# The ternary feed-forward stage of an eight-layer kernel: the batch loop written out, both middle layers with output tiles innermost, each batch's last layer issued between the next batch's first tiles

## The chip, the cores and the metric

One core of one Trainium2 chip runs the whole program once. The metric is the device time of that one launch in microseconds (us); lower is better. The data type of every matmul in the stage at hand is fp32.

## What is computed

The program is a sequence of eight layers with a residual and a layernorm behind each: four attention-like layers and four feed-forward layers, on x of 4 batches of 512 positions with 128 channels. The stage that the diff touches is the second of the eight, the first feed-forward (its weights are -1, 0 or 1 times a factor, but are used here as plain fp32):

```python
def _tlin(x, w, s):
    return jnp.einsum('bsi,oi->bso', x, w) * s
h = jax.nn.silu(_tlin(x, w1_w, w1_s)) * _tlin(x, w2_w, w2_s)     # 128 -> 512
h = jax.nn.gelu(_tlin(h, h1_w, h1_s), approximate=False)         # 512 -> 512
h = jax.nn.gelu(_tlin(h, h2_w, h2_s), approximate=False)         # 512 -> 512
return _tlin(h, w3_w, w3_s)                                      # 512 -> 128
...
x = _layernorm(x + _L0_ffn_ref(x, ...), axis=-1)
```

## The kernel before

`build` (at the end of the file) runs the stages one behind another; each stage is a block of its own in which every engine has one instruction stream, and a block ends when all its engines are done. Between two stages stands `layernorm`, a block too, in which SyncE also loads the next stage's weights. So the ternary stage begins when the layernorm before it has written X, and the next layernorm begins when the ternary stage has written the last batch of R.

Channels lie on the 128 partitions and the 512 positions of a batch along the free dimension. X is the stage's input and also the residual, R its output. The 512 hidden channels are four tiles of 128 (`HT` is 4), counted by m for an output tile and by k for an input tile. PSUM is `c.ps`, eight banks of 128x512 fp32; every matmul fills one bank with 128x512.

For each batch b, in a `Fori` loop on each of three engines (L182, L206, L221):

- First layers (L187, L188): for m = 0 to 3 one matmul with w1 into bank 2m and one with w2 into bank 2m+1. ScalarE takes the silu of bank 2m into G (L209), and VectorE multiplies bank 2m+1 by its scale and by G into H1 (L225).
- First middle layer (L195, `layer` 0): TensorE waits for all four H1 tiles, and then makes output tile m by four matmuls over k in a row, into bank m. ScalarE takes the gelu of each output tile into H2 (L214).
- Second middle layer (L195 again, `layer` 1): TensorE waits for all four H2 tiles; output tile m goes to bank 4+m, its gelu to H3 (L214).
- Last layer (L200): TensorE waits for all four H3 tiles; four matmuls over k into bank 0. VectorE scales this and adds X into R (L228). The next batch's first matmul writes bank 0, and so TensorE waits for L228 (the wait at the top of its loop, which for batch 0 is satisfied by the `sem_inc` at L219).

That makes 8 + 16 + 16 + 4 = 44 matmuls a batch and 176 in the stage. The order of each engine is the order of the program text; nothing is planned or reordered. Semaphore `tiles` counts finished output tiles of TensorE, `act_done` ScalarE's activations, `dve_done` VectorE's products; in the loops their target values are computed from the loop's register b. SyncE's part in the stage is four DMAs that write blanks into `da_bands` (L176) for the stage that follows.

The relative attention (its first block entry below is L1700) and the other attention stages don't share code with this one. `hashed_ffn`, `lowrank_ffn` and others are written without `Fori`; `rwkv_attention` has one.

Of the kernel before, what the change touches and what calls it, by code (L numbers as in the profile page):

```python
# [15 lines left out]
ALU = mybir.AluOpType  # L16
# [3 lines left out]
P = 128  # L20
B, T = 4, 512
N = B * T
PAD = 3
# [119 lines left out]
def ternary_ffn(c):  # L143

    d = c.dram
    H = 512
    HT = H // P
    loaded, tiles = c.sem("tf_loaded"), c.sem("tf_tiles")
    act_done, dve_done = c.sem("tf_act_done"), c.sem("tf_dve_done")
    TILES, ACTS, DVES = 2 * HT + 2 * HT + 1, 3 * HT, HT + 1  # L150
    SPAN, ROW = 64, 256
    c.bands = [[c.nc.dram_tensor(f"da_bands{i}{j}", (UNITS * P * ROW,), F32, kind="Internal").ap() for j in range(2)] for i in range(2)]
    with ExitStack() as ctx:
        w1 = c.sb("tf_w1", [P, H], ctx)
        w2 = c.sb("tf_w2", [P, H], ctx)
        h1 = c.sb("tf_h1", [P, HT, H], ctx)
        h2 = c.sb("tf_h2", [P, HT, H], ctx)
        w3 = c.sb("tf_w3", [P, HT, P], ctx)
        s = c.sb("tf_s", [P, 4 * HT + 1], ctx)
        G = c.sb("tf_G", [P, HT, T], ctx)  # L160
        H1 = c.sb("tf_H1", [P, HT, T], ctx)
        H2 = c.sb("tf_H2", [P, HT, T], ctx)
        H3 = c.sb("tf_H3", [P, HT, T], ctx)
        pairs = [(w1[:, :], d["tf_w1"]), (w2[:, :], d["tf_w2"]), (s[:, :], d["tf_s"]), (h1[:, :, :], d["tf_h1"]),
                 (h2[:, :, :], d["tf_h2"]), (w3[:, :, :], d["tf_w3"])]
        yield [(loaded, pairs)]
        block = c.block(ctx)

        @block.sync
        def _(eng):  # L170
            eng.wait_ge(loaded, 16 * len(pairs))
            blank = c.X[:, 0, PAD + T:PAD + T + SPAN].unsqueeze(1).to_broadcast([P, UNITS, SPAN])
            for pair in c.bands:
                for side, buf in enumerate(pair):
                    dst = bass.AP(buf.tensor, buf.offset + (ROW - SPAN) * side, [[ROW, P], [P * ROW, UNITS], [1, SPAN]])
                    eng.dma_start(dst, blank).then_inc(loaded, 16)  # L176
            eng.wait_ge(loaded, 16 * (len(pairs) + 4))

        @block.tensor
        def _(eng):  # L180
            eng.wait_ge(loaded, 16 * len(pairs))
            with eng.Fori(0, B) as b:  # L182
                x = c.X[:, b, PAD:PAD + T]
                eng.wait_ge(dve_done, b * DVES + 1)
                for m in range(HT):
                    cols = slice(m * P, (m + 1) * P)
                    eng.matmul(c.ps[:, 2 * m, :], w1[:, cols], x, start=True, stop=True).then_inc(tiles, 1)  # L187
                    eng.matmul(c.ps[:, 2 * m + 1, :], w2[:, cols], x, start=True, stop=True).then_inc(tiles, 1)  # L188
                eng.wait_ge(dve_done, b * DVES + HT + 1)
                for layer, (w, hid) in enumerate(((h1, H1), (h2, H2))):  # L190
                    if layer:
                        eng.wait_ge(act_done, b * ACTS + 2 * HT)
                    for m in range(HT):
                        for k in range(HT):
                            mm = eng.matmul(c.ps[:, 4 * layer + m, :], w[:, k, m * P:(m + 1) * P], hid[:, k, :],  # L195
                                            start=k == 0, stop=k == HT - 1)
                        mm.then_inc(tiles, 1)
                eng.wait_ge(act_done, b * ACTS + 3 * HT)
                for k in range(HT):
                    mm = eng.matmul(c.ps[:, 0, :], w3[:, k, :], H3[:, k, :], start=k == 0, stop=k == HT - 1)  # L200
                mm.then_inc(tiles, 1)

        @block.scalar
        def _(eng):
            eng.wait_ge(loaded, 16 * len(pairs))
            with eng.Fori(0, B) as b:  # L206
                for m in range(HT):
                    eng.wait_ge(tiles, b * TILES + 2 * m + 1)
                    eng.activation(G[:, m, :], c.ps[:, 2 * m, :], ACT.Silu, scale=s[:, m:m + 1]).then_inc(act_done, 1)  # L209
                for layer, out in enumerate((H2, H3)):  # L210
                    for m in range(HT):
                        eng.wait_ge(tiles, b * TILES + 2 * HT + layer * HT + m + 1)
                        k = (2 + layer) * HT + m
                        eng.activation(out[:, m, :], c.ps[:, 4 * layer + m, :], ACT.Gelu, scale=s[:, k:k + 1])\  # L214
                           .then_inc(act_done, 1)

        @block.vector
        def _(eng):
            eng.sem_inc(dve_done, 1)  # L219
            eng.wait_ge(loaded, 16 * len(pairs))  # L220
            with eng.Fori(0, B) as b:  # L221
                for m in range(HT):
                    eng.wait_ge(tiles, b * TILES + 2 * m + 2)
                    eng.wait_ge(act_done, b * ACTS + m + 1)
                    eng.scalar_tensor_tensor(H1[:, m, :], c.ps[:, 2 * m + 1, :], s[:, HT + m:HT + m + 1], G[:, m, :],  # L225
                                             ALU.mult, ALU.mult).then_inc(dve_done, 1)
                eng.wait_ge(tiles, b * TILES + TILES)
                eng.scalar_tensor_tensor(c.R[:, b, :], c.ps[:, 0, :], s[:, 4 * HT:4 * HT + 1], c.X[:, b, PAD:PAD + T],  # L228
                                         ALU.mult, ALU.add).then_inc(dve_done, 1)


def hashed_ffn(c):
# [2438 lines left out]


LAYERS = [delta_attention, ternary_ffn, relative_attention, hashed_ffn, rwkv_attention, lowrank_ffn, rotary_attention, routed_ffn]


# [155 lines left out]
```

## Time and profile before

| what | value |
|---|---|
| median of 3 runs | 3025.05 us (3017.87 to 3030.14) |
| the profiled execution's own time | 3023.27 us |
| its span | 3021.3 us |
| mean granted TensorE clock over the span | 0.867 |
| TensorE busy over the whole span | 2375.7 us, 79% |
| VectorE, ScalarE busy | 2157.8 us, 1549.6 us |
| the ternary stage, first matmul to last residual | 1343.7 to 1516.5 us |

The span is the time between the first and the last instruction that the profile shows; the execution's own time is 2.0 us above it. All positions below are in us from the span's start. "PE" is TensorE's matmul, "PEld" its weight load, "DVE" VectorE, "ACT" ScalarE, and PEq or DVEq the instruction queue of an engine, where register and semaphore instructions are seen. One fp32 matmul of the source appears as two MATMUL instructions (two passes), each with its weight load, so the 44 matmuls of a batch are 88 passes.

### The profile page before, as it was taken

To read this page: it belongs to the slowest core of one execution; us is meant where nothing else is said; L and a number is where in the kernel's file an instruction comes from. 1 tells how busy PE (TensorE), PEld (TensorE's weight loads), DVE (VectorE), ACT (ScalarE), POOL (GpSimd) and SP (SyncE) were. 2 spreads that over 40 slices of the span, in tenths; PEclk is the share of its full clock that TensorE was granted. 3 is DMA by queue.
4 is the path that set the end of the run, shared out by engine and by line. 5 is a ranking of instruction groups with operands and counts; after the bars stand their busy time and mean duration, and the time that the engine had idled before them with its cause. 6 is when DMAs were issued, how large, how long until landed. Compare 5 with 4: busy or idle time off the path is not lost. (4 is left out here: it accounts for less than half of the span.)

```text
span 3021.3 us, 63536 instructions
## 1 busy us (share of the span) xinstructions
PE 2375.7 (79%) x25313; PEld 1626.9 (54%) x25365; DVE 2157.8 (71%) x3992; ACT 1549.6 (51%) x3982; POOL 270.2 (9%) x280
## 2 busy tenths in 40 slices
PE   6778877787777877769938999998867766778677
PEld 5667777676676766743315666665322221222366
DVE  6999999999999999940035777787256656665465
ACT  3555555566556656652235777776311132556434
POOL 0000000000000000000031010100022311110242
PEclk9887788888887878889968999999988887999888
DMA  5111110111111111020039999994100001110421
GB/s 174 30 30 30 30 30 23 24 30 30 30 30 30 30 30 30 16 67 0 0 89 232 246 231 239 238 236 119 35 0 0 0 23 57 40 40 26 156 70 63
DMA packets 200035, 214.28 MB, mean 71 GB/s; under 512 B 32150, under 2 KB 185766, under 8 KB 194310
## 3 DMA queue, kind: packets, MB, share of 16 engines
q1 hardware_dynamic: 197353, 205.39, 25.9%
q0 software_dynamic: 2400, 4.95, 0.5%
q8 instruction: 199, 3.26, 0.5%
q14 instruction: 83, 0.68, 0.1%
HBM read 138.16 MB, written 74.74 MB: 70 GB/s over the span
## 5 line engine op out<-in xcount | busy, mean ns | idle before, releaser
L1274 DVE TENSOR_REDUCE ra_top<-ps 128x1 f32<-128x512 f32 x256 | 161.1, 683 | 97.7 <-PE ps L1078 91.3
L2594 DVE TENSOR_REDUCE dl_ZO<-dl_XP 128x64 f32<-128x128 f32 (+6 forms) x448 | 219.7, 490 | 15.4
L2590 DVE TENSOR_TENSOR dl_XP<-dl_ZO,dl_G 128x64 f32<-128x64 f32 (+6 forms) x448 | 194.6, 434 | 15.4
L1772 ACT ACTIVATE da_AB<-ps 128x384 f32<-128x384 f32 x256 | 124.5, 490 | 147.0 <-PE ps L1634 143.4
L1195 ACT ACTIVATE ra_PT<-ps 128x512 f32<-128x512 f32 x256 | 136.6, 598 | 117.3 <-PE ps L1097 116.6
L1928 DVE TENSOR_TENSOR ps<-ps,da_window 128x192 f32<-128x192 f32 (+1 forms) x256 | 101.2, 395 | 122.3 <-PE ps L1657 118.0
L1782 ACT ACTIVATE da_E<-ps,da_top 128x512 f32<-128x512 f32 x256 | 176.1, 688 | 17.4 <-DVE da_top L1931 16.9
L1931 DVE TENSOR_REDUCE da_top<-ps 128x1 f32<-128x512 f32 x256 | 177.0, 691 | 8.8
L1664 PE MATMUL ps<-ident,da_E 128*128 128x128 f32 x1024 | 169.1, 288 | 1.3 <-ACT da_E L1782 1.2
L2165 PE MATMUL ps<-X,dl_taps_q 128*128 128x128 f32 x1088 | 148.9, 304 | 2.2 <-DVE dl_taps_q L2655 2.2
L2165 PEld LDWEIGHTS ps<-X,dl_taps_q 128*128 128x128 f32 x1088 | 145.7, 220 | 4.2 <-DVE dl_taps_q L2655 2.4
L2223 PE MATMUL ps<-dl_kqN,dl_ST 64*64 64x32 f32 x4096 | 114.6, 282 | 40.4 <-DVE dl_ST L2614 36.6
L1473 POOL MEMSET da_K<- 32x4096 f32 x2 | 7.1, 3573 | 1528.9 <-POOLq L82 1528.9
L2165 PE MATMUL ps<-X,dl_taps_k 128*128 128x128 f32 x1088 | 143.1, 297 | 0.0
L2165 PEld LDWEIGHTS ps<-X,dl_taps_k 128*128 128x128 f32 x1088 | 140.0, 213 | 1.0
L1664 PEld LDWEIGHTS ps<-ident,da_E 128*128 128x128 f32 x1024 | 108.4, 141 | 50.4 <-issue 39.9
L2223 PEld LDWEIGHTS ps<-dl_kqN,dl_ST 64*64 64x64 f32 x4096 | 109.9, 210 | 46.0 <-issue 45.6
L2165 PEld LDWEIGHTS ps<-X,dl_taps_v 128*128 128x128 f32 x1088 | 126.1, 193 | 13.1 <-issue 9.5
L2431 ACT ACTIVATE dl_FB<-dl_F,dl_beta_now 128x32 f32<-128x32 f32 x512 | 126.7, 351 | 9.8 <-DVE dl_F L2499 9.8
L2165 PE MATMUL ps<-X,dl_taps_v 128*128 128x128 f32 x1088 | 126.0, 275 | 3.3 <-DVE dl_taps_v L2655 2.3
L2581 DVE TENSOR_TENSOR dl_ZO<-dl_ZO,dl_aT 128x32 f32<-128x32 f32 (+6 forms) x448 | 128.0, 286 | 0.0
L1078 PE MATMUL ps<-ra_KS,ra_QS 128*128 128x512 bf16 x246 | 103.3, 424 | 23.3 <-DMA ra_QS<-ra_zero 22.7
(403 smaller groups left out, 5766.6 us busy)
## 6 DMA issues: line engine op xcount, KB each, us to landing
da_bands<-da_AB SPq DMA_DIRECT2D x128, 384.0 KB, 3.8
dl_Abc<-dl_ends SPq DMA_DIRECT2D x64, 512.0 KB, 6.3
da_window<-da_bands SPq DMA_DIRECT2D x128, 192.0 KB, 4.4
da_across<-da_bands SPq DMA_DIRECT2D x128, 192.0 KB, 4.5
da_parts<-da_split SPq DMA_DIRECT2D x64, 96.0 KB, 3.3
rf_We<-in_rf_We SPq DMA_DIRECT2D x1, 4608.0 KB, 23.0
da_K<-da_parts SPq DMA_DIRECT2D x16, 256.0 KB
da_Q<-da_parts SPq DMA_DIRECT2D x16, 256.0 KB
```

Of the source, the lines that this page charges most:

```text
L1195: eng.activation(PT[:, k % 2, h, :], ps[:, tscore_bank(UNITS * m + v), :], ACT.Exp).then_inc(s["exps"], 1)
L1274: eng.tensor_reduce(top[:, m % 2, u:u + 1], ps[:, score_bank(UNITS * m + u), :], AXX, ALU.max, negate=True).then_inc(s["maxima"], 1)
L1664: mm = eng.transpose(ps[:, 2 + U % 2, k * P:(k + 1) * P], E[:, U % 2, k * P:(k + 1) * P], c.ident[:, :])
L1772: eng.activation(AB[:, j % STAGES, h, :, :], ps[:, band_bank(v), 0:2 * BAND].rearrange("p (k x) -> p k x", k=2), ACT.Copy)\
L1782: eng.activation(E[:, U % 2, :], ps[:, score_bank(U), :], ACT.Exp, bias=top[:, u:u + 1], accum_out=total[:, m % 2, u:u + 1]).then_inc(s["e ...
L1931: eng.tensor_reduce(top[:, u:u + 1], bank, AXX, ALU.max, negate=True).then_inc(s["maxima"], 1)
L2165: mm = eng.matmul(out, taps[w][:, tap, cols], columns_of(c.X, m, tap), start=tap == 0, stop=tap == TAPS - 1)
L2223: mm = eng.matmul(starts_ps[e][DK * (h ^ w):DK * (h ^ w) + DK, w, pair // 2, :], ST[rows, pair, :], kqN[rows, pair, e * CH:(e + 1) * CH, : ...
L2431: ins = eng.activation(FB[:, e, :, t // SB, t % SB], F[:, e, :, t // SB, t % SB], ACT.Copy, scale=beta_now[:, 1, t:t + 1])
L2581: link(eng.tensor_tensor(mine[:, :, 0:t], mine[:, :, 0:t], aT[:, e, :, u, t + 1].unsqueeze(2).to_broadcast([P, I, t]), ALU.mult))
L2590: link(eng.tensor_tensor(XP[:, :, :, SB - t:], seen.unsqueeze(1).to_broadcast([P, 2, I, t + 1]), G[:, x:x + 2, keys][:, ::-1, :].unsqueeze ...
L2594: link(eng.tensor_reduce(ZO[:, to:to + 1 + (2 * I - 1) * CH:CH].rearrange("p (k i) -> p k i", k=2), XP[:, :, :, SB - 1 - t:], AXX, ALU.add))
```

## The change

The batch loop of all three engines is a Python loop now, so it is written out four times, and every wait has a constant, looked up in the tables `tile`, `acts` and `dves` that are filled in the order in which the engines issue. In the two middle layers the loop over k is the outer one and the loop over the output tiles m the inner one: all four banks of a layer are open at once, each gets its matmul of k = 0, then each that of k = 1, and so on, and the wait stands ahead of each k. The first layers' tiles are taken in the order 0, 1, 3, 2. The last layer of batch b-1 is issued behind the first layers' tiles 0 and 1 of batch b, into bank 4 instead of bank 0, and its residual likewise on VectorE; tile 2 of the first layers, whose banks are 4 and 5, stands behind a wait for that residual.

```diff
--- before.py
+++ after.py
@@ -147,7 +147,22 @@
     HT = H // P
     loaded, tiles = c.sem("tf_loaded"), c.sem("tf_tiles")
     act_done, dve_done = c.sem("tf_act_done"), c.sem("tf_dve_done")
-    TILES, ACTS, DVES = 2 * HT + 2 * HT + 1, 3 * HT, HT + 1
+    ORDER = (0, 1, 3, 2)
+    tile, acts, dves = {}, {}, {}
+    for b in range(B):
+        for m in ORDER:
+            if m == 3 and b:
+                tile["out", b - 1] = len(tile) + 1
+                dves["out", b - 1] = len(dves) + 1
+            for side in range(2):
+                tile["first", b, m, side] = len(tile) + 1
+            acts["silu", b, m] = len(acts) + 1
+            dves["gated", b, m] = len(dves) + 1
+        for layer in range(2):
+            for m in range(HT):
+                tile["hidden", b, layer, m] = len(tile) + 1
+                acts["gelu", b, layer, m] = len(acts) + 1
+    tile["out", B - 1] = len(tile) + 1
     SPAN, ROW = 64, 256
     c.bands = [[c.nc.dram_tensor(f"da_bands{i}{j}", (UNITS * P * ROW,), F32, kind="Internal").ap() for j in range(2)] for i in range(2)]
     with ExitStack() as ctx:
@@ -178,55 +193,71 @@
 
         @block.tensor
         def _(eng):
+            def first(b, m):
+                cols = slice(m * P, (m + 1) * P)
+                for side, w in enumerate((w1, w2)):
+                    eng.matmul(c.ps[:, 2 * m + side, :], w[:, cols], c.X[:, b, PAD:PAD + T], start=True, stop=True).then_inc(tiles, 1)
+
+            def hidden(b, layer, w, hid, ks):
+                for i, k in enumerate(ks):
+                    if layer == 0:
+                        eng.wait_ge(dve_done, dves["gated", b, ks[max(i, 1)]])
+                    else:
+                        eng.wait_ge(act_done, acts["gelu", b, 0, k])
+                    for m in range(HT):
+                        mm = eng.matmul(c.ps[:, 4 * layer + m, :], w[:, k, m * P:(m + 1) * P], hid[:, k, :], start=i == 0, stop=i == HT - 1)
+                        if i == HT - 1:
+                            mm.then_inc(tiles, 1)
+
+            def last(b):
+                eng.wait_ge(act_done, acts["gelu", b, 1, HT - 1])
+                for k in range(HT):
+                    mm = eng.matmul(c.ps[:, 4, :], w3[:, k, :], H3[:, k, :], start=k == 0, stop=k == HT - 1)
+                mm.then_inc(tiles, 1)
+
             eng.wait_ge(loaded, 16 * len(pairs))
-            with eng.Fori(0, B) as b:
-                x = c.X[:, b, PAD:PAD + T]
-                eng.wait_ge(dve_done, b * DVES + 1)
-                for m in range(HT):
-                    cols = slice(m * P, (m + 1) * P)
-                    eng.matmul(c.ps[:, 2 * m, :], w1[:, cols], x, start=True, stop=True).then_inc(tiles, 1)
-                    eng.matmul(c.ps[:, 2 * m + 1, :], w2[:, cols], x, start=True, stop=True).then_inc(tiles, 1)
-                eng.wait_ge(dve_done, b * DVES + HT + 1)
-                for layer, (w, hid) in enumerate(((h1, H1), (h2, H2))):
-                    if layer:
-                        eng.wait_ge(act_done, b * ACTS + 2 * HT)
-                    for m in range(HT):
-                        for k in range(HT):
-                            mm = eng.matmul(c.ps[:, 4 * layer + m, :], w[:, k, m * P:(m + 1) * P], hid[:, k, :],
-                                            start=k == 0, stop=k == HT - 1)
-                        mm.then_inc(tiles, 1)
-                eng.wait_ge(act_done, b * ACTS + 3 * HT)
-                for k in range(HT):
-                    mm = eng.matmul(c.ps[:, 0, :], w3[:, k, :], H3[:, k, :], start=k == 0, stop=k == HT - 1)
-                mm.then_inc(tiles, 1)
+            for b in range(B):
+                for m in ORDER:
+                    if m == 3 and b:
+                        last(b - 1)
+                    if m == 2 and b:
+                        eng.wait_ge(dve_done, dves["out", b - 1])
+                    first(b, m)
+                hidden(b, 0, h1, H1, ORDER)
+                hidden(b, 1, h2, H2, range(HT))
+            last(B - 1)
 
         @block.scalar
         def _(eng):
             eng.wait_ge(loaded, 16 * len(pairs))
-            with eng.Fori(0, B) as b:
-                for m in range(HT):
-                    eng.wait_ge(tiles, b * TILES + 2 * m + 1)
+            for b in range(B):
+                for m in ORDER:
+                    eng.wait_ge(tiles, tile["first", b, m, 0])
                     eng.activation(G[:, m, :], c.ps[:, 2 * m, :], ACT.Silu, scale=s[:, m:m + 1]).then_inc(act_done, 1)
                 for layer, out in enumerate((H2, H3)):
                     for m in range(HT):
-                        eng.wait_ge(tiles, b * TILES + 2 * HT + layer * HT + m + 1)
+                        eng.wait_ge(tiles, tile["hidden", b, layer, m])
                         k = (2 + layer) * HT + m
                         eng.activation(out[:, m, :], c.ps[:, 4 * layer + m, :], ACT.Gelu, scale=s[:, k:k + 1])\
                            .then_inc(act_done, 1)
 
         @block.vector
         def _(eng):
-            eng.sem_inc(dve_done, 1)
+            def residual(b):
+                eng.wait_ge(tiles, tile["out", b])
+                eng.scalar_tensor_tensor(c.R[:, b, :], c.ps[:, 4, :], s[:, 4 * HT:4 * HT + 1], c.X[:, b, PAD:PAD + T],
+                                         ALU.mult, ALU.add).then_inc(dve_done, 1)
+
             eng.wait_ge(loaded, 16 * len(pairs))
-            with eng.Fori(0, B) as b:
-                for m in range(HT):
-                    eng.wait_ge(tiles, b * TILES + 2 * m + 2)
-                    eng.wait_ge(act_done, b * ACTS + m + 1)
+            for b in range(B):
+                for m in ORDER:
+                    if m == 3 and b:
+                        residual(b - 1)
+                    eng.wait_ge(tiles, tile["first", b, m, 1])
+                    eng.wait_ge(act_done, acts["silu", b, m])
                     eng.scalar_tensor_tensor(H1[:, m, :], c.ps[:, 2 * m + 1, :], s[:, HT + m:HT + m + 1], G[:, m, :],
                                              ALU.mult, ALU.mult).then_inc(dve_done, 1)
-                eng.wait_ge(tiles, b * TILES + TILES)
-                eng.scalar_tensor_tensor(c.R[:, b, :], c.ps[:, 0, :], s[:, 4 * HT:4 * HT + 1], c.X[:, b, PAD:PAD + T],
-                                         ALU.mult, ALU.add).then_inc(dve_done, 1)
+            residual(B - 1)
 
 
 def hashed_ffn(c):
```

## Rows read from the trace of the kernel before

**Rows 1.** Page of the profile: span, TensorE over the span.
```profile
span 3021.3 us, 63536 instructions
PE 2375.7 (79%) x25313; PEld 1626.9 (54%) x25365; DVE 2157.8 (71%) x3992; ACT 1549.6 (51%) x3982; POOL 270.2 (9%) x280
```
**Rows 2.** Busy time by window: window, length, then busy us and (instructions); PEclk granted clock.
```profile
1343.70:1349.80 6.10, 6.08 (x8) 2.51 (x9) 0.75 (x1) 2.30 (x3) 0.00 (x0) 0.51 0.86 193
1474.10:1516.70 42.60, 38.83 (x88) 16.39 (x88) 3.75 (x5) 9.53 (x13) 0.00 (x0) 1.00 0.00 0
```
**Rows 3.** Waits, 1330 to 1530: who waited for whom, total us, times, longest.
```profile
DVE R L228 <- PE ps L200: 134.3, 4, 33.6
ACT tf_H L214 <- PE ps L195: 95.1, 32, 3.8
PE ps L187 <- DVEq L219: 5.9, 1, 5.9
PE ps L1700 <- PEq L82: 5.5, 1, 5.5
```
**Rows 4.** Timeline, all engines, batch 0 to batch 1: start, length, instruction, idle before.
```profile
1343.72 2.07 PE L187 MATMUL ps<-X,tf_w 128*128 x2 [5.86 <-DVEq L219]
...
1352.80 1.02 PE L188 MATMUL ps<-X,tf_w 128*128 x2
...
1354.75 14.00 PE L195 MATMUL ps<-tf_H,tf_h 128*128 128x512 f32 x32 [0.93 <-DVE tf_H L225]
...
1383.57 0.69 ACT L214 ACTIVATE tf_H<-ps,tf_s 128x512 f32<-128x512 f32 x1 [2.75 <-PE ps L195]
1384.27 1.28 ACT L209 ACT_TABLE_LOAD   x1
1384.31 3.70 PE L200 MATMUL ps<-tf_H,tf_w 128*128 128x512 f32 x8 [0.78 <-ACT tf_H L214]
1388.28 0.75 DVE L228 SCALAR_TENSOR_TENSOR R<-ps,tf_s,X 128x512 f32 x1 [33.59 <-PE ps L200]
1389.19 1.12 PE L187 MATMUL ps<-X,tf_w 128*128 x2 [1.18 <-DVE R L228]
```
**Rows 5.** Timeline, TensorE, end of batch 2, batch 3 and the exit.
```profile
1469.29 3.70 PE L200 MATMUL ps<-tf_H,tf_w 128*128 128x512 f32 x8 [0.78 <-ACT tf_H L214]
1474.14 1.12 PE L187 MATMUL ps<-X,tf_w 128*128 x2 [1.16 <-DVE R L228]
1475.10 1.02 PE L188 MATMUL ps<-X,tf_w 128*128 x2
...
1480.25 1.02 PE L188 MATMUL ps<-X,tf_w 128*128 x2
1482.20 14.00 PE L195 MATMUL ps<-tf_H,tf_h 128*128 128x512 f32 x32 [0.93 <-DVE tf_H L225]
1496.98 14.00 PE L195 MATMUL ps<-tf_H,tf_h 128*128 128x512 f32 x32 [0.78 <-ACT tf_H L214]
1511.76 3.70 PE L200 MATMUL ps<-tf_H,tf_w 128*128 128x512 f32 x8 [0.78 <-ACT tf_H L214]
1515.71 0.75 DVE L228 SCALAR_TENSOR_TENSOR R<-ps,tf_s,X 128x512 f32 x1 [33.57 <-PE ps L200]
```
**Rows 6.** Timeline, TensorE, recurrent stage: spread (L826) and gather (L830) matmuls in turn.
```profile
2290.35 1.02 PE L830 MATMUL ps<-rw_rS,rw_gather 128*128 128x512 f32 x2
2291.20 1.02 PE L826 MATMUL ps<-rw_rkv,rw_spread 128*128 128x512 f32 x2
2292.06 1.02 PE L830 MATMUL ps<-rw_rS,rw_gather 128*128 128x512 f32 x2
```
**Rows 7.** Busy time by window, in three stages that are written out.
```profile
500.00:520.00 20.00, 15.69 (x419) 14.89 (x422) 18.78 (x38) 7.70 (x29) 0.00 (x0) 0.84 0.01 2
2114.70:2118.00 3.30, 3.25 (x4) 1.50 (x5) 0.00 (x0) 1.12 (x1) 0.00 (x0) 0.54 0.00 0
2463.00:2466.00 3.00, 3.00 (x5) 1.01 (x3) 1.47 (x2) 0.00 (x0) 0.00 (x0) 0.52 0.00 0
```

## What the change does to the time, predicted before it was run

> **What bounds the kernel now.** I read the page first: TensorE is busy 79% of the span [rows 1], but that is a mean over eight stages, so it says nothing of this one. The windows over the stage come next: a batch takes some 42.5 us and TensorE is busy for 38.83 of them, VectorE for 3.75 and ScalarE for 9.5 to 10.8 [rows 2] (batches 1 and 2 have the same numbers as batch 3). TensorE is the engine that sets the end, and the other two have room for a delay of many microseconds. The waits name large sums, 134.3 us of VectorE and 95.1 us of ScalarE [rows 3]; these are idle times of engines that don't bound, and they cost nothing. What costs is the short list of waits in which TensorE stands, and the timeline shows where: four times a batch, always where one layer needs the last tile of the layer before.
>
> **The unit.** In a run of first-layer passes 12 passes go from 1475.10 to 1480.25 [rows 5], 0.429 us each. The stage's 88 passes a batch are 37.75 us of the 42.5; the rest, 4.7 us, is stall. I measure every stall as start of a phase to start of the next, less the phase's passes at 0.429, so that the slightly longer first pass behind a stall is counted with it.
>
> **What goes away, stall by stall.**
> 1. First layers to first middle layer. Batch 3: 1474.14 to 1482.20 is 8.06, less 16 passes (6.86) is 1.20 [rows 5]. In batch 0 the last pair starts at 1352.80, its slot ends at 1353.66, and the next phase starts at 1354.75: 1.09 [rows 4]. Four of them: 1.09 + 3 x 1.20 = 4.69. Afterwards this layer begins with k = 0, whose product comes two tiles earlier, and needs the last-made tile (k = 2) only after 24 passes or 10.3 us.
> 2. First to second middle layer: 1482.20 to 1496.98 is 14.78, less 32 passes (13.73) is 1.05 [rows 5]. Four: 4.20. With m innermost the output tiles are finished in the last four matmuls, 0.86 apart. ScalarE's gelu takes 0.69 [rows 4], so it keeps up; tile 0's gelu ends some 1.7 us before the last tile is done (3 x 0.86 earlier, plus 0.2 and 0.69), and the next layer starts without a pause. The gelu of tile 3 is needed 12 matmuls (10.3 us) later.
> 3. Second middle layer to last layer: again 14.78, 1.05 [rows 5]. Three of the four go, as the last layer of batch b-1 stands behind four matmuls (3.43 us) of batch b; that of batch 3 has no next batch and stays.
> 4. Last layer to the next batch. From 1384.31 to 1389.19 is 4.88, less 8 passes (3.43) is 1.45 [rows 4]; from 1469.29 to 1474.14 it is 1.42 [rows 5]. With 1.43 between them for the middle one, three make 4.30. This is the wait for the residual L228, which reads bank 0.
>
> Sum 4.69 + 4.20 + 3.15 + 4.30 = 16.3 us. The other way round: from 1353.66 there remain 336 passes, 144.1 us, plus one stall of 1.05; from the start of the last phase to the end of the residual it is 1511.76 to 1516.46, 4.70 [rows 5]. The residual would end at 1353.66 + 144.1 - 3.43 + 1.05 + 4.70 = 1500.1 instead of 1516.5, which is 16.4. I take 16.4.
>
> **Two small terms.** TensorE's idle time at the entry of the stage is 5.86 us, released by the queue of VectorE (the `sem_inc`), and 5.5 at the relative attention, a block without a loop [rows 3]; the layernorm before both is the same code. Without loop and `sem_inc` the entry should be 0.36 shorter. Its bounds are 0 and 0.36 and I take 0.36, since the row is the same code but for the loop. The residual starts 0.25 behind the end of the last pass (1511.76 + 3.70 to 1515.71) [rows 5], with register operations of the loop in between; I count 0.1 for these, between 0 and 0.25.
>
> **What is added, and what hides it.**
> - The residual of batch b-1 is now waited for ahead of tile 2. It ends 4.72 us after its last layer starts (1384.31 to 1389.03) [rows 4]; on TensorE the last layer (8 passes) and tile 3 (4 passes) take 12 x 0.429 = 5.15 us. That leaves 0.43 us, just one pass, by which a weight load runs ahead. So it is late by 0 to 0.1 us, three times: 0 to 0.3, and I take 0. Behind the waiting instruction stand only the batch's own tile 2 and its first middle layer.
> - ScalarE switches its table between gelu and silu, 1.28 us [rows 4]. The first silu of batch b can come no earlier than gelu, table and silu behind the second middle layer: about 0.2 + 0.69 + 1.28 + 0.69 = 2.9 us. Its product is needed at 10.3 us behind that point, so this is hidden; without cover it would cost its 1.28 once a batch.
> - The last layer waits for the gelu of tile 3, done about 1 us behind the second middle layer and needed 3.43 us behind it: 2.4 us of room.
> - Nothing is added in passes, weight loads or bytes. SyncE's four DMAs are untouched.
> - The written-out stream is longer. A written-out stage gives TensorE 419 matmuls in 20 us [rows 7], over 20 a microsecond, where this one needs 2.3. Its bounds are 0 and, as the loop's step back ends in a first matmul only 0.15 us behind the residual (1389.04 to 1389.19) [rows 4], a gain or loss of that size at each of three seams, 0.45 us. I take 0, as the denser stream is the nearer row.
> - Four open accumulation groups instead of one. The recurrent stage changes bank with each matmul while the gather in bank 2 (L830, `start=k == 0`) is still open: 2290.35, 2291.20, 2292.06, that is 0.86 for two passes, the same as within one bank [rows 6]. So 0, and no gain is possible either, as the passes are back to back already. The row has one open group and not four, which leaves rival C.
> - The clock at the entry. TensorE had been idle for 5.86 us and runs at 0.51 of full speed, the 1.2 GHz level, until about 1349.8, 6.1 us [rows 2]. Behind the same layernorm the hashed stage has 0.54 for only 3.3 us, and the low-rank stage is at 0.52 over 3 us after earlier slow ones [rows 7]. When it rises after the change can't be told from these rows; the stretch could be 3 us shorter, which gives 1.5 us back, or as much longer. I take 0.
>
> **A page that speaks against it.** The timeline shows gaps of 0.78 to 1.2 us in this stage and a granted clock of 1.00 for all of batch 3 [rows 2, 5]. The Trainium skill (TensorE: Matmul & The Clock Gate, section Loop structure matters more than you think) holds that the loop over k for one output tile should be the inner one so that TensorE stays warm, with the waits of the bad order being for DMAs of 8 us. The trace does not bear it out for this stage: there is no DMA in the loops, and the nest before kept its clock through all these gaps. What it would do here is rival E.
>
> **Sum.** 16.4 + 0.4 + 0.1 = 16.9 us off 3023.3, the profiled execution's own time (span 3021.3, [rows 1], and 2.0 around it): 3006.4. That execution was 1.8 below the median of the runs, so against the median 3025.05 the forecast is 3008.2, or -0.56%. All of it should reach the end: the next layernorm can't start before the last residual, and no transfer of the next stage is awaited there.
>
> **Rivals.**
> - A. Half of the stalls come back elsewhere: the residual wait is late and each last layer still stalls, so that stalls 3 and 4 (7.45 us) stay. For it: only 0.43 us of room. Against: the residual's own duration is fixed. 3008.2 + 7.5 = 3015.7.
> - B. The stage gives all of it, but the stages behind it give some back: they start 17 us earlier, with other clock and DMA phases. For it: runs of the very same program lie 12.3 us apart; against it: nothing in those stages refers to a fixed time. About half the spread, 6 to 10 us: 3014 to 3018.
> - C. Slower: with four groups open and the bank changing at each matmul, the weight load is no longer hidden behind the pass before. Its place is the 256 passes of the middle layers. A weight load takes 16.39 / 88 = 0.19 us [rows 2], so the price is 256 x 0.19 = 48.6 us, 3008.2 + 48.6 = 3057. It decides from 16.9 / 256 = 0.066 us a pass. For it: no row has four open groups. Against it: the alternating passes of [rows 6].
> - D. The change doesn't do what it says at the seam of the middle layers: the stall only moves, because the gelu of tile 0 is not done when the second middle layer starts. The room is 1.7 us, against it; for it speaks only that the gelus now come in a burst. Then 1.05 us stays four times: 3012.4.
> - E. TensorE falls to its 1.2 GHz level in the middle layers. A pass costs 0.429 more, 256 of them 110 us: 3118, and 39 such passes take the gain away. Against it: 1.00 granted in spite of larger gaps [rows 2]. The rule of the Trainium skill told above would make the time this.
>
> **Numbers.** Forecast 78%, A 6%, B 9%, C 2%, D 4%, E 1%. What a measurement can tell from no change is 0.5%, 15.1 us, so the line lies at 3009.9, only 1.7 us above the forecast, and three runs of the kernel before spread over 12.3 us. With some 5 us of scatter in the difference the forecast comes out below the line in 64% of its cases, 0.50; A, B and D give another 0.05. Faster 0.55. Slower 0.04: C and E, and 0.01 for a drift in the stages behind beyond B. Same 0.41. The range takes 5 to 6 us of scatter and the clock's 1.5 on the low side, and A, B and D on the high side: 3000 to 3019.
>
> **What would show it.** In the trace of the changed kernel: the middle layers' passes in one unbroken run of 0.429 each, also across the seam of the two; TensorE's idle time between 1354 and the last layer of batch 3 near 0, with one gap of 0.78 left in front of that last layer; entry idle 5.5; about 42.5 - 4.7 = 37.8 us a batch at a clock of 1.00; first matmul to last residual about 156.2 us instead of 172.7. The argument is wrong if passes in the middle layers take more than 0.43, if the clock falls below 1.00 inside the stage, or if a gap remains ahead of tile 2. It is right in the stage and wrong in the sum if the stage takes 156 us and the span is still above 3012.

## The result and the profile after

The changed kernel took 3004.43 us (median of six runs, 2997.9 to 3005.43), the kernel before 3025.66 us (3017.87 to 3032.14, also six): a ratio of 0.9926 with a 95% interval of 0.9908 to 0.9945, or 17 to 28 us less. The forecast was 3008.2 in a range of 3000 to 3019. The profiled execution has a span of 3003.6 us, 17.7 below the one before. Of all executions in this text one stands apart, an execution of e9 that took 5431 us; no trace of it exists, and the ratios leave it out.

The windows over the stage in the changed kernel (window, length, busy us of PE, PEld, DVE, ACT and POOL, granted clock, DMA share, GB/s) answer to [rows 2]. From the second window on TensorE is busy all the time, but for 1.9 us of the last one, where 38.83 of 42.6 us was the rule before. The granted clock is 0.50 at the entry and 1.00 from the first middle layer on:

```profile
1342.50:1346.00 3.50, 3.44 (x4) 1.50 (x5) 0.00 (x0) 1.30 (x2) 0.00 (x0) 0.50 0.66 148
1346.00:1349.80 3.80, 3.80 (x10) 1.77 (x9) 1.50 (x2) 2.04 (x3) 0.00 (x0) 0.96 0.88 199
1385.00:1426.80 41.80, 41.80 (x98) 18.43 (x98) 5.16 (x7) 11.96 (x16) 0.00 (x0) 1.00 0.00 0
1426.80:1464.60 37.80, 37.80 (x89) 16.72 (x88) 3.66 (x5) 10.74 (x15) 0.00 (x0) 1.00 0.00 0
1464.60:1498.00 33.40, 31.51 (x74) 13.56 (x73) 1.50 (x2) 7.03 (x11) 0.00 (x0) 1.00 0.00 0
```

The timeline of TensorE shows the two middle layers as one run of 64 passes, with no idle time behind it in three of four batches. From the start of such a run to the start of the next one on it takes 27.46 us (1351.36 to 1378.82), 0.429 a pass; the 27.63 of the line hold the last pass to its end. One gap is left, of 0.78 us, ahead of the last layer of batch 3; compare [rows 4, 5], where such a line stands at each change of layer. (The times are start and length; L199 is the first layers, L208 the middle ones, L215 the last.)

```profile
1342.56 8.96 PE L199 MATMUL ps<-X,tf_w 128*128 128x512 f32 x16 [5.50 <-PEq L82]
1351.36 27.63 PE L208 MATMUL ps<-tf_H,tf_h 128*128 128x512 f32 x64
1378.82 3.60 PE L199 MATMUL ps<-X,tf_w 128*128 128x512 f32 x8
1382.26 3.60 PE L215 MATMUL ps<-tf_H,tf_w 128*128 128x512 f32 x8
1385.69 3.60 PE L199 MATMUL ps<-X,tf_w 128*128 128x512 f32 x8
1389.12 27.63 PE L208 MATMUL ps<-tf_H,tf_h 128*128 128x512 f32 x64
...
1464.66 27.63 PE L208 MATMUL ps<-tf_H,tf_h 128*128 128x512 f32 x64
1493.06 3.70 PE L215 MATMUL ps<-tf_H,tf_w 128*128 128x512 f32 x8 [0.78 <-ACT tf_H L241]
1497.87 3.67 PE L95 MATMUL ps<-R,ones_mean 128*128 128x512 f32 x8 [1.11 <-PEq L168]
```

The same boundary on ScalarE and VectorE (L241 gelu, L236 silu, L258 product, L248 residual) shows what now runs while TensorE works. The gelus follow one another 0.86 us apart, the table switch comes while TensorE is in tiles 0 and 1, and the residual ends at 1386.64, before TensorE needs it for tile 2, four passes behind 1385.69, at 1387.41:

```profile
1378.16 0.69 ACT L241 ACTIVATE tf_H<-ps,tf_s 128x512 f32<-128x512 f32 x1 [0.17 <-PE ps L208]
1379.02 0.69 ACT L241 ACTIVATE tf_H<-ps,tf_s 128x512 f32<-128x512 f32 x1 [0.17 <-PE ps L208]
1379.73 1.28 ACT L236 ACT_TABLE_LOAD   x1
1381.02 1.26 ACT L236 ACTIVATE tf_G<-ps,tf_s 128x512 f32<-128x512 f32 x2
1385.89 0.75 DVE L248 SCALAR_TENSOR_TENSOR R<-ps,tf_s,X 128x512 f32<-128x512 f32 x1 [2.67 <-PE ps L215]
```

The waits over the same stretch (who waited for whom, total us, times, longest) answer to [rows 3]. VectorE's and ScalarE's large sums are still there, one of them under a new name (93.1 us for the silu), and cost as little as before:

```profile
DVE tf_H L258 <- ACT tf_G L236: 93.1, 4, 29.5
ACT tf_H L241 <- PE ps L208: 86.1, 32, 10.5
PE ps L199 <- PEq L82: 5.5, 1, 5.5
PE ps L215 <- ACT tf_H L241: 0.8, 1, 0.8
```

Cut at the first matmul of each layernorm (L95), the two profiled executions fall into nine parts (us):

| part | before | after |
|---|---|---|
| up to the first layernorm | 1330.76 | 1329.95 |
| **ternary stage with the layernorm ahead of it** | **186.02** | **167.92** |
| relative attention | 585.37 | 585.16 |
| hashed feed-forward | 67.88 | 69.75 |
| recurrent stage | 273.09 | 273.10 |
| low-rank stage | 24.46 | 24.78 |
| rotary attention | 348.23 | 344.85 |
| routed stage | 188.38 | 190.90 |
| last layernorm and store | 17.11 | 17.19 |

The ternary segment lost 18.1 us. The others moved by up to 3.4 us either way; in sum they are 0.4 us longer.

### The profile page after: what moved, and what is told of

It is laid out like the page before. It is cut to its first block and busy times, and to the rows that moved or that the text cites. A ratio compares the mean times of both kernels' runs of the same rounds, so it can differ in the third digit from the quotient of the medians.

```text
span 3003.6 us, 63465 instructions
## 1 busy us (share of the span) xinstructions
PE 2375.6 (79%) x25365; PEld 1622.7 (54%) x25365; DVE 2157.1 (72%) x3992; ACT 1550.6 (52%) x3982; POOL 270.3 (9%) x280
## 5 line engine op out<-in xcount | busy, mean ns | idle before, releaser
L2625 DVE TENSOR_REDUCE dl_ZO<-dl_XP 128x64 f32<-128x128 f32 (+6 forms) x448 | 219.7, 490 | 15.4
L2621 DVE TENSOR_TENSOR dl_XP<-dl_ZO,dl_G 128x64 f32<-128x64 f32 (+6 forms) x448 | 194.7, 435 | 15.4
L2254 PE MATMUL ps<-dl_kqN,dl_ST 64*64 64x32 f32 x4096 | 108.0, 273 | 42.1 <-DVE dl_ST L2645 37.1
L2254 PEld LDWEIGHTS ps<-dl_kqN,dl_ST 64*64 64x64 f32 x4096 | 103.2, 198 | 47.9 <-issue 47.7
L1128 PE MATMUL ps<-ra_QS,ra_KS 128*128 128x512 bf16 x256 | 98.7, 396 | 32.3 <-DMA ra_QS<-ra_notes 28.0
```

The source lines that it names most:

```text
L2254: mm = eng.matmul(starts_ps[e][DK * (h ^ w):DK * (h ^ w) + DK, w, pair // 2, :], ST[rows, pair, :], kqN[rows, pair, e * CH:(e + 1) * CH, : ...
L2621: link(eng.tensor_tensor(XP[:, :, :, SB - t:], seen.unsqueeze(1).to_broadcast([P, 2, I, t + 1]), G[:, x:x + 2, keys][:, ::-1, :].unsqueeze ...
L2625: link(eng.tensor_reduce(ZO[:, to:to + 1 + (2 * I - 1) * CH:CH].rearrange("p (k i) -> p k i", k=2), XP[:, :, :, SB - 1 - t:], AXX, ALU.add))
```

## Experiments

Each kernel was timed against the kernel before on one chip: the first four together, the next four together, the last three together. A difference in us that is given with an interval is the ratio's, taken of the median before; it differs by up to 3 us from the difference of the two medians. Lengths from the traces stand beside it, since the time of an execution scatters by several us and the stage behind its first phase by 0.01. "Behind the first phase" is the stage from the end of the first layers of batch 0 to the end of the last residual; it leaves out the first phase, whose length hangs on the clock. "Segment" is the part of the table above.

| kernel | ratio to before, 95% interval | first phase | behind it | segment |
|---|---|---|---|---|
| before (first trace) | | 9.94 | 162.80 | 186.02 |
| after (first timing) | 0.9926, 0.9908 to 0.9945 | 8.80 | 146.19 | 167.92 |
| e5_control | 1.0002, 0.9990 to 1.0013 | 8.64 | 162.80 | 184.72 |
| e1_written_out | 1.0009, 0.9997 to 1.0021 | 8.92 | 161.29 | 183.13 |
| e2_m_inner | 0.9972, 0.9961 to 0.9984 | 8.71 | 152.66 | 174.29 |
| e3_deferred | 0.9985, 0.9975 to 0.9995 | 9.94 | 154.83 | 179.23 |
| e4_as_changed | 0.9957, 0.9943 to 0.9971 | 8.66 | 146.19 | 167.78 |
| e6_no_cover | 0.9945, 0.9932 to 0.9957 | 8.50 | 149.34 | 170.76 |
| e7_last_by_k | 0.9947, 0.9933 to 0.9960 | 9.95 | 145.15 | 169.58 |
| e8_later | 1.0001, 0.9993 to 1.0010 | 8.64 | 146.19 (without the added matmuls) | 184.99 |
| e9_clock_kept | 0.9930, 0.9917 to 0.9944 | 6.95 | 145.15 | 165.02 |
| e10_as_changed | 0.9941, 0.9927 to 0.9955 | 8.77 | 146.20 | 167.88 |
| e11_written_out | 1.0001, 0.9992 to 1.0010 | 8.39 | 161.29 | 182.61 |

**e1_written_out** (and e11, the same kernel). The changed kernel with its `ORDER` as 0 to 3, k inside in the middle layers, and the last layer and its residual at the end of their own batch, in bank 0:

```diff
-ORDER = (0, 1, 3, 2)
+ORDER = (0, 1, 2, 3)
...
-                for i, k in enumerate(ks):
-                    if layer == 0:
-                        eng.wait_ge(dve_done, dves["gated", b, ks[max(i, 1)]])
-                    else:
-                        eng.wait_ge(act_done, acts["gelu", b, 0, k])
-                    for m in range(HT):
+                if layer == 0:
+                    eng.wait_ge(dve_done, dves["gated", b, ORDER[-1]])
+                else:
+                    eng.wait_ge(act_done, acts["gelu", b, 0, HT - 1])
+                for m in range(HT):
+                    for k in range(HT):
...
                 hidden(b, 1, h2, H2, range(HT))
-            last(B - 1)
+                last(b)
```

> Only the batch loop written out with constant waits; tile order, loop nests, bank 0 and the place of the last layer as in the kernel before. Theory (the gain is the removed stalls, term by term): the four stalls of each batch stay, only the entry (0.36 us) and the register operations ahead of the residual (0.1 to 0.2 us, four times) go; the stage, first matmul to end of last residual, is 172 us (171 to 173, by the clock at the entry), and the time is 0.5 to 1.5 us below the kernel before. Rival (the written-out stream itself gives the surplus of some 4 us over the forecast sum): the time is 4 to 5 us below the kernel before, outside the stage too.

Behind the first phase the stage is 1.5 us shorter, more than expected; with a first phase of 8.92 it takes 170.2 us, below the 171 to 173 that were expected. The trace shows where: the gaps are the ones of before, but shorter. Ahead of the middle layer TensorE is idle for 0.84 or 0.85 us instead of 0.93, and behind the last layer, where the residual is awaited, 0.84 instead of 1.16 to 1.18 [rows 4, 5]. Ahead of the second middle layer and of the last layer, where ScalarE's gelu is awaited, it is 0.78 in both kernels. The next lines are from e1, batch 1, with the residual of batch 0 ahead of them:

```profile
1382.40 0.75 DVE L243 SCALAR_TENSOR_TENSOR R<-ps,tf_s,X 128x512 f32<-128x512 f32 x1 [33.35 <-PE ps L212]
1383.21 7.13 PE L197 MATMUL ps<-X,tf_w 128*128 128x512 f32 x16 [0.84 <-DVE R L243]
1391.19 14.00 PE L206 MATMUL ps<-tf_H,tf_h 128*128 128x512 f32 x32 [0.84 <-DVE tf_H L251]
1405.96 14.00 PE L206 MATMUL ps<-tf_H,tf_h 128*128 128x512 f32 x32 [0.78 <-ACT tf_H L236]
1420.74 3.70 PE L212 MATMUL ps<-tf_H,tf_w 128*128 128x512 f32 x8 [0.78 <-ACT tf_H L236]
```

The timing did not follow: +2.7 us (-0.9 to +6.4), with the two medians 0.5 us apart the other way (3035.03 against 3035.53), where the segment has -1.6 against the control and -2.9 against the first trace. The rival's 4 to 5 us are not there.

**e2_m_inner.** As e1, but both middle layers as in the changed kernel, so that from that kernel it differs by `ORDER`, the bank, the wait for the residual (ahead of the batch's first matmul, as in e1) and this:

```diff
                 hidden(b, 1, h2, H2, range(HT))
-            last(B - 1)
+                last(b)
```

> Written out, and output tiles innermost in both middle layers; the last layer stays at the end of its own batch, bank 0. Theory: stalls 1 and 2 go (4.69 + 4.20 = 8.9 us), stalls 3 and 4 stay (1.05 x 4 and 1.4 x 3); with the two small terms some 9.5 to 10 us below the kernel before, and gaps in TensorE only ahead of and behind each last layer. Rival (the two parts need each other, since the residual of the last layer is the longest stall and takes up what the nest gives): under 5 us. Rival C of the forecast: passes of the middle layers above 0.43 us.

Stalls 1 and 2 are gone, 3 and 4 stay, as this stretch of its TensorE timeline shows; the 64 passes take 27.63 us to the end of the last one, as in the changed kernel, so four open groups cost nothing. Against e1 the stage is 8.63 us shorter, and 10.1 against the kernel before. The rival of under 5 us is out by the stage; the time is 8.5 us lower (4.8 to 11.8).

```profile
1389.16 27.63 PE L206 MATMUL ps<-tf_H,tf_h 128*128 128x512 f32 x64
1417.57 3.70 PE L213 MATMUL ps<-tf_H,tf_w 128*128 128x512 f32 x8 [0.78 <-ACT tf_H L237]
1422.11 7.13 PE L197 MATMUL ps<-X,tf_w 128*128 128x512 f32 x16 [0.84 <-DVE R L244]
```

**e3_deferred.** The changed kernel with the middle layers of e1 (k inside, one wait for the layer).

> Written out, order of tiles 0, 1, 3, 2 and the last layer behind the next batch's first tiles as in the changed kernel, but both middle layers with k innermost and one wait ahead of the layer as before. Theory: stalls 3 and 4 go (3.15 + 4.30 = 7.45 us), stalls 1 and 2 stay; with the two small terms some 8 to 8.5 us below the kernel before. Rival: the residual wait ahead of tile 2 is late and shows as a gap there, under 5 us in all.

Stalls 3 and 4 are gone and no gap stands ahead of tile 2, which is in the second L199 line:

```profile
1408.53 14.00 PE L208 MATMUL ps<-tf_H,tf_h 128*128 128x512 f32 x32 [0.78 <-ACT tf_H L240]
1422.37 3.60 PE L199 MATMUL ps<-X,tf_w 128*128 128x512 f32 x8
1425.80 3.59 PE L214 MATMUL ps<-tf_H,tf_w 128*128 128x512 f32 x8
1429.23 3.60 PE L199 MATMUL ps<-X,tf_w 128*128 128x512 f32 x8
1433.68 14.00 PE L208 MATMUL ps<-tf_H,tf_h 128*128 128x512 f32 x32 [0.85 <-DVE tf_H L257]
```

Behind the first phase it is 6.46 us shorter than e1 and 8.0 shorter than before, as the theory had it. The time is only 4.6 us lower (1.5 to 7.6), which by itself would have spoken for the rival; the trace decides against it. Its first phase was 9.94 us in the profiled execution, as slow as in the first trace, while that of the control was 8.64; what it was in the other executions is not known.

The three add up: 1.51 (written out) + 8.63 (nest) + 6.46 (deferred) = 16.60, and the changed kernel has 162.80 - 146.19 = 16.61. Neither part needs the other.

**e4_as_changed and e10_as_changed.** The changed kernel again, on the chip of e1 to e3 and on that of e9.

> The changed kernel once more, on the same chip as the three parts. Theory: 16.9 us below the kernel before by the forecast's sum and 18 by the stage in its trace (0.37 and 0.6 us of it being the faster rise of the clock and a shorter exit), so a ratio of 0.9940 to 0.9944. Rival: the stages behind answer to an earlier start too, and the median is 21 to 22 us lower as in the first timing, ratio 0.9926 to 0.993.

> The changed kernel a third time, beside the next and the one before on one chip. Theory (the forecast's sum plus the clock and the shorter exit, 16.9 to 18.2 us; what the first two timings showed around it, -22 and -13 us, is scatter of the stages outside): ratio 0.9940 to 0.9945. Rival (the spread is of kernels, not of timings): again outside 0.993 to 0.9957.

With the first timing there are three: -22, -13 and -18 us, -17.8 in the mean; the medians give -21.2, -14.2 and -18.9. e4 gained less than either theory had (0.9957); e10 lies in the theory's band. Behind the first phase e4 has 146.19, to the hundredth what the first trace has. Of the 1.2 us by which the segment beats the forecast's 16.9, the expectation gave the clock 0.37 and the exit 0.6; by the traces it is 1.14 and 0.1.

**e5_control.** The kernel before, timed as if it were changed.

> The kernel before itself, once more, timed as if it were a changed one and profiled on the same chip as the next three. It gives the stage (172.7 us, first matmul to end of last residual, by the first trace) and the stages outside it for a like-for-like sum. Expected of any theory: ratio 1.000 within 0.0012, and a first phase of the stage between 8.6 and 10 us by the clock.

Ratio 1.0002. Its stage is 171.44 us and not 172.7, and all of the 1.30 us stands in the first phase, 8.64 instead of 9.94 [rows 4]: here the full clock came two matmuls earlier, as the next lines of the control's TensorE timeline show. The first pair is slow, the second nearly, and the third at 1.02 us has full speed; in the first trace it was the fifth.

```profile
1343.20 2.07 PE L187 MATMUL ps<-X,tf_w 128*128 x2 [5.86 <-DVEq L219]
1345.06 1.78 PE L188 MATMUL ps<-X,tf_w 128*128 x2
1346.68 1.02 PE L187 MATMUL ps<-X,tf_w 128*128 x2
```

The stages outside the segment take 2849.9 us on this chip against 2835.3 in the first trace; most of it is in the routed stage, 205.1 against 188.4. So spans of different chips are not to be compared here, and no sum in this text does it; only the ternary stage itself, which agrees to 0.01 us behind its first phase, is compared across chips.

**e6_no_cover.**

```diff
-                    if m == 3 and b:
+                    if m == 0 and b:
                         last(b - 1)
```

(the same for its residual and in the tables; the wait for the residual stays ahead of tile 2).

> The changed kernel with the last layer of batch b-1 issued straight behind its second middle layer, ahead of tiles 0 and 1 of batch b; the residual is still waited for only ahead of tile 2. Theory (two tiles in front of the last layer are what hides the gelu of tile 3): stall 3 of 1.05 us comes back three times, 3.2 us, as a gap of 0.78 in front of each last layer, and no gap behind it; the segment from layernorm to layernorm grows from 167.9 to 171.1 us. Rival (the gelu is done in time in any case, since tiles are now finished 0.86 us apart): no gap, 167.9.

The gap of 0.78 is back ahead of every last layer, and none is behind:

```profile
1418.05 3.70 PE L215 MATMUL ps<-tf_H,tf_w 128*128 128x512 f32 x8 [0.78 <-ACT tf_H L241]
1421.59 7.03 PE L199 MATMUL ps<-X,tf_w 128*128 128x512 f32 x16
```

149.34 - 146.19 = 3.15 us, which is stall 3 as it was priced. The two tiles in front are what hides the gelu. (The segment is 170.76 and not 171.1, as the first phase is 8.50 here against 8.80.)

**e7_last_by_k.**

```diff
-                eng.wait_ge(act_done, acts["gelu", b, 1, HT - 1])
                 for k in range(HT):
+                    eng.wait_ge(act_done, acts["gelu", b, 1, k])
```

> The changed kernel with a wait ahead of each k of the last layer, for the gelu of that k alone, instead of one wait for the gelu of tile 3. Theory: the one stall that is left, ahead of the last layer of batch 3, goes (1.05 us), as k = 0 to 2 take 2.6 us and the gelu is done 1 us in; the segment is 166.9 us and TensorE has no gap in the stage. Rival (the four waits cost TensorE something in the three seams where they were satisfied anyhow): no shorter than 167.9. The median can't tell 1 us; the trace can.

The last gap is gone (the last L208 run ends in the slot before 1493.54, and L215 follows with no idle time), 146.19 becomes 145.15, 1.04 us. The rival is out: the three other seams are as long as before (3.43 or 3.44 us from the start of the last layer to the next). But this execution's first phase was 9.95 us, and its segment of 169.58 is longer than that of the changed kernel: the slow entry took more than the wait gave. The segment was the wrong measure to put into the expectation.

```profile
1466.08 27.63 PE L208 MATMUL ps<-tf_H,tf_h 128*128 128x512 f32 x64
1493.54 3.60 PE L215 MATMUL ps<-tf_H,tf_w 128*128 128x512 f32 x8
```

**e8_later.**

```diff
             last(B - 1)
+            for n in range(21):
+                eng.matmul(c.ps[:, 0, :], w1[:, 0:P], c.X[:, 0, PAD:PAD + T], start=True, stop=True)
```

> The changed kernel with 21 more matmuls (42 passes, 18.0 us) of TensorE behind its last one, whose results nobody reads, so that the stage ends some 17 us later, as in the kernel before, but with the written-out stream. Theory (the stages behind don't care when they start): the time is that of the kernel before within its scatter, ratio 0.999 to 1.001, and the segments behind the stage are those of the changed kernel. Rival (the stages behind answer to their start time or to the written-out stream): the ratio differs from that of the changed kernel plus 17 us by 3 us or more, with the difference in the segments behind the stage.

The added passes run without a gap behind the last layer:

```profile
1492.33 18.20 PE L230 MATMUL ps<-X,tf_w 128*128 128x512 f32 x42
```

The segment is 184.99, 0.3 us from the control's, and the ratio is 1.0001 (0.9993 to 1.0010). Giving the 17 us back in the place where they were won gives the time of the kernel before, so the written-out stream, which is in this kernel too, costs the other stages nothing that 3 us would show. Against e6 and e7 on the same chip the segment is 14.2 and 15.4 us longer and the median 16.1 and 16.3. Had the stages behind given back 6 to 10 us of an earlier start, the medians would differ by that much less; this tells against rival B. An effect of 2 us is not ruled out: the routed stage takes 206.6 and 207.8 us in the traces of e6 and e7, which start it earlier, against 205.1 and 204.9 in the control and e8. On the chip of e9 to e11 it does not go with the start (187.4, 190.8 and 192.3 us, the latest start having the longest), and each is a single execution.

**e9_clock_kept.** As e7, and in six of the layernorms:

```diff
+            for n in range(5 if base // B in (0, 1, 2, 3, 5, 6) else 0):
+                eng.matmul(c.ps[:, 0, :], c.ones_mean[:, :], c.R[:, 0, :], start=True, stop=True)
```

> The kernel with the wait by k in the last layer (as e7_last_by_k), and in six of the eight layernorms five more matmuls (10 passes, 4.3 us at full clock) of TensorE behind its last useful one, results unread, into bank 0, which is free by then. They fill most of the 5.5 us that TensorE stands idle before each next stage. Theory (the first phase of the stage takes 8.5 to 10.1 us instead of 6.86 only because the clock has fallen to its 1.2 GHz level in that idle time): the first phase takes 6.9 us, the stage 152 us, its segment 165 us, and other stages that begin with dense matmuls gain 1 to 3 us each: 5 to 12 us below the changed kernel in all. Rival (the clock falls anyhow in the last microsecond of idle, or the later stages wait for DMAs and VectorE at their start): only the ternary stage gains, or nothing; ratio to the kernel before as that of the changed kernel.

In the ternary stage it did what its theory says: the first phase is 6.95 us and the stage 152.1. In its TensorE timeline the added matmuls (L100) end 1.21 us before the stage begins:

```profile
1338.01 4.46 PE L100 MATMUL ps<-R,ones_mean 128*128 128x512 f32 x10
1343.67 7.11 PE L201 MATMUL ps<-X,tf_w 128*128 128x512 f32 x16 [1.21 <-PEq L82]
```

The windows over the first 6 us of the ternary and of the hashed stage in e9 have a granted clock of 1.00:

```profile
1343.67:1349.67 6.00, 6.00 (x14) 2.73 (x15) 1.97 (x3) 3.24 (x4) 0.00 (x0) 1.00 0.79 178
2095.80:2101.80 6.00, 6.00 (x14) 2.72 (x15) 1.98 (x3) 3.23 (x4) 0.00 (x0) 1.00 0.01 3
```

The same windows in e10, the changed kernel on the same chip, have 0.69 and 0.57:

```profile
1342.34:1348.34 6.00, 6.00 (x10) 2.69 (x11) 1.22 (x2) 2.66 (x3) 0.00 (x0) 0.69 0.69 158
2095.17:2101.17 6.00, 5.99 (x8) 2.54 (x9) 0.75 (x1) 2.54 (x3) 0.00 (x0) 0.57 0.00 0
```

So the hashed stage gained too (66.41 us against 68.98). Of the others with added matmuls ahead of them the rotary stage is the same (344.62 against 344.80), the routed one 3.4 us shorter (187.40 against 190.81), the relative attention 2.2 longer (587.11 against 584.94) and the recurrent one 4.0 longer (278.66 against 274.70); why the last two are longer is open, and all four are single executions. The stages outside the segment come to 2835.9 against 2835.4 us in sum, so the 5 to 12 us that the theory had for the whole did not come. Its ratio, 0.9930, is 3.3 us below that of e10 on the same chip, with intervals that overlap; it has the lowest median of this study (2999.97 of all six executions, 2999.36 without the one of 5431 us, against 3002.51), but is not shown to be faster than the changed one.

**e11_written_out.**

> The written-out kernel without the two other parts once more, since its first timing (+2.7 us, -0.9 to +6.4) and its segment (-2.9 us) disagree. Theory (scatter between timings): 2 to 3 us below the kernel before, ratio 0.9990 to 0.9994. Rival (a written-out stream costs the rest of the program 3 to 5 us): ratio 1.0005 to 1.0015 again.

+0.3 us (-2.4 to +3.0), between the two; the median is 1.0 us below. The segment is 182.61. Together with e1 the written-out kernel is not measurably faster than the one before, although its trace is 1.5 us shorter behind the first phase. Whether 2 us are lost elsewhere or only in the scatter is not settled; e8, with the same kind of stream, shows no such loss.

## Why the prediction was right

- **The unit and the four stalls.** Forecast 16.4 us of stalls and 0.1 at the last residual. Measured behind the first phase: 16.6 us in the first trace and in e4, of which 0.2 are at the last residual. Passes stayed at 0.429 us with four groups open, so rival C has no place, and the granted clock was 1.00 from the first middle layer on, so rival E has none. The section of the Trainium skill that E was taken from (TensorE: Matmul & The Clock Gate, Loop structure matters more than you think) sets a wait for a DMA ahead of every matmul in its bad nest; it does not say what k outermost does without such a wait, so E was priced from a wider reading than the page gives. Rival D doesn't either: all four seams between the middle layers are without a gap.
- **How they divide.** The forecast gave stalls 1 and 2 8.9 us and stalls 3 and 4 7.45. Taken one by one on the written-out kernel they are 8.63 and 6.46; the missing 0.3 and 1.0 are in the 1.5 us of writing out. The forecast had counted only 0.1 us for the loop's register operations, at the last residual, where 0.2 went. Writing out took 0.08 to 0.09 us from each gap ahead of the first middle layer and 0.32 to 0.34 from each behind a last layer, and nothing from the gaps behind ScalarE's gelus. In the sum it makes no difference, as these stalls are removed whole.
- **The entry.** 0.36 us forecast from the blocks without a loop; 5.86 became 5.50.
- **The clock at the entry.** Taken as 0 with 1.5 us either way. The first phase went from 9.94 to 8.80, 1.14 us, and this is the rest of the 18.1 us of the segment: 16.6 + 0.36 + 1.14. So the stage took 155.0 us from its first matmul to its last residual, where 156.2 were forecast. That the 1.14 fell on this side is luck and need not be the change's doing: the kernel before itself had 8.64 in the control, and across the kernels without e9 the phase lies between 8.39 and 9.95.
- **The residual wait.** The room was put at 0.43 us; it was 0.77, as the residual starts 0.2 us sooner behind its matmul and the last layer, no longer behind a stall, starts without a longer first pass, 0.1 us. Rival A has no place.
- **The cover by tiles 0 and 1.** Forecast 2.4 us of room; the trace has 2.55 (the gelu ends at 1379.71, the last layer starts at 1382.26), and e6 shows the cover and its price of 3.15 us.
- **From the stage to the median.** The forecast was -16.9, the first timing -22 (17 to 28), or -21.2 by the medians. The 4 to 5 us between them come from no part that could be found: the trace has 18.1 in the segment and 0.4 against it elsewhere, a second and a third timing gave -13 and -18, and e8 finds no 6 to 10 us of rival B. The stage's part of the result is not luck; on which side of the forecast the first timing fell is. The intervals of the first and of the second timing overlap only between 0.9943 and 0.9945, and what makes one timing differ from another by that much stays open. Stages that the diff doesn't touch do scatter by as much: outside the segment the four traces of e5 to e8, on one chip, have 2845.0 to 2851.2 us.

The chance of "faster by over 0.5%" was put at 0.55 because the forecast stood 1.7 us beyond the line. Of three timings, two are beyond it and one (0.9957) is not; that hesitation was right.

## What to carry to other kernels

Where one engine is busy nearly all of a stage, list its own waits only, and measure each from phase start to phase start in units of its pass; the sum of stalls got in that way was right to 0.1 us here, while the waits of the other engines are large and worth nothing. A wait for the last tile of a layer goes without any extra buffer if the consumer's loop over its inputs is the outer one and each of its output tiles has a PSUM bank of its own; where no such loop helps, work of the next batch in front of the waiting layer does: two tiles hid a gelu, and without them 1.05 us a time came back. A gain near the scatter of the median is better shown by the trace of the stage, less the part that the clock moves, and by giving the same time back in the same place, than by the timing alone.

## What the runs showed of the hardware that was not expected

- Waits in a register loop cost something in front of VectorE and nothing in front of ScalarE. Written out, VectorE started its residual 0.04 us behind the listed end of TensorE's last pass instead of 0.25, and the product ahead of a middle layer 0.04 instead of 0.13; TensorE started the next batch 0.06 us behind the residual instead of 0.15 (e1 against the kernel before). TensorE's idle time behind ScalarE's gelus, with waits of the same kinds, was 0.78 us in both. The loop's step, its register addresses and its computed wait values went together, and no run tells them apart.
- The length of the slow stretch at the entry of a stage differs between executions of the same kernel: the first phase took 9.94 and 8.64 us for the kernel before, from 8.39 to 9.95 over all but e9, and 6.95 when TensorE was kept busy through most of the idle time ahead of it. This is as much as a whole stall of the kind removed here.
- Chips can differ in one stage only: the routed stage took 187.4 to 192.3 us in the first two traces and in the three on the chip of e9 to e11, and 204.7 to 207.8 in all eight traces on the two others. Whether it is the chip or something else that differed between those timings is open.
